# The opening of a four-layer residual chain: token columns and codebook spread by TensorE, lora_A in two loads, lora_B turned into every eighth column

## The reference

```python
x = x + (x @ W0.T + b0 + coeff[:, None, None] * einsum('bsi,bio->bso', x, 2 * mask - 1))
delta = lora_B @ lora_A * 0.5                  # lora_B 1024x64, lora_A 64x1024
cb = codebook / max(abs(codebook))             # 8 levels
normalized = (weight + delta) / exp(scale_log) # by groups of 128 columns
quantized = cb[searchsorted(thresholds, normalized)]
x = x + x @ (quantized * exp(scale_log) + delta).T
x = x + x @ W2.T + b2 + (x @ A2[tok2]) @ B2[tok2] * 2
x = x + (x @ B3[tok3].T) @ A3[tok3].T
```

## Time and profile before

| | us |
|---|---|
| median of 3 runs (lowest to highest) | 549.82 (549.53 to 550.76) |
| profiled execution, its own time | 549.87 |
| its span, first to last instruction | 548.2 |
| PE busy in the span | 533.4 (97%) |
| DVE busy | 468.8 (86%) |
| ACT busy | 341.7 (62%) |
| POOL busy | 192.9 (35%) |

### The profile page before, as it was taken

The page is one execution under the profiler, slowest core; times in us unless marked ns, Lnnn a source line. Parts: engine busy times, 40 slices in busy tenths (PEclk is TensorE's granted clock), DMA queues, the critical chain, the costliest instruction groups (busy, mean ns, idle before and its releaser), DMA issues.

```text
span 548.2 us, 8917 instructions
## 1 busy us (share of the span) xinstructions
PE 533.4 (97%) x2856; PEld 454.1 (83%) x2856; DVE 468.8 (86%) x723; ACT 341.7 (62%) x658; POOL 192.9 (35%) x179
## 2 busy tenths in 40 slices
PE   5999999999999999999999999999999999999997
PEld 4988888888888787887888788788888878878886
DVE  5998898988865879977999989998997998999862
ACT  3777776776745874586566657557566665755720
POOL 2669867987734020012034204111410420411130
PEclk9999999999999999999999999999999999999999
DMA  8766041843486995558456545645835654664122
GB/s 232 244 92 148 21 125 48 248 138 115 102 186 189 348 326 100 189 157 171 138 161 167 123 160 175 114 155 189 172 134 168 167 126 158 180 103 168 61 59 77
DMA packets 145261, 84.06 MB, mean 153 GB/s; under 512 B 102672, under 2 KB 118032, under 8 KB 145104
## 3 DMA queue, kind: packets, MB, share of 16 engines
q1 hardware_dynamic: 143312, 78.97, 52.4%
q0 software_dynamic: 1632, 4.72, 3.4%
q10 hardware_dynamic: 288, 0.01, 0.0%
HBM read 67.43 MB, written 16.25 MB: 153 GB/s over the span
## 4 chain that ended last, share of the span: by engine, by line
PE 83%; DVE 9%; ACT 4%; DMA 3%; issue 1%; POOL 0%; DVEq 0%; ACTq 0%; SPq 0%; POOLq 0%
PE bank L1637 19%; PE bank L1644 10%; PE bank L1676 7%; PE bank L1677 7%; PE bank L1675 7%; PE bank L1511 5%; PE bank L1513 5%; PE bank L1512 5%; PE bank L1726 3%; PE bank L1725 3%; PE bank L1727 3%; PE bank L1691 3%; PE bank L1421 2%; PE bank L1704 1%; DVE w_lo L1074 1%; DVE merged_ring L1168 1%
## 5 line engine op out<-in xcount | busy, mean ns | idle before, releaser
L1637 PE MATMUL bank<-x_t_pair,m_hi 128*128 128x512 f32 x512 | 128.5, 393 | 1.5 <-ACT m_hi L800 1.4
L800 ACT CAST m_hi<-merged_ring 128x512 fp32r<-128x512 f32 x128 | 73.1, 619 | 60.7 <-PE bank L1644 31.9
L1637 PEld LDWEIGHTS bank<-x_t_pair,m_hi 128*128 128x128 f32 x512 | 92.5, 189 | 19.2 <-ACT m_hi L800 2.3
L1174 DVE TENSOR_TENSOR m_lo<-merged_ring,m_hi 128x512 fp32r<-128x512 f32 x128 | 86.3, 720 | 12.5 <-ACT m_hi L800 12.2
L576 POOL TENSOR_TENSOR x_t_pair<-x_sum,x_t_pair 128x256 fp32r<-128x256 f32 x32 | 29.7, 960 | 179.1 <-ACT x_t_pair L861 179.1
L1168 DVE TENSOR_TENSOR merged_ring<-merged_ring,w_t 128x1024 f32<-128x1024 f32 x64 | 82.1, 1311 | 11.3 <-ACT merged_ring L790 10.3
L790 ACT ACTIVATE merged_ring<-mask_ring,batch_now 128x1024 f32<-128x1024 int32 x64 | 78.0, 1241 | 21.1 <-DMA mask_ring<-in_mask_Bx4096x_ik 20.3
L1644 PEld LDWEIGHTS bank<-x_t_pair,m_lo 128*128 128x128 f32 x512 | 69.8, 190 | 5.0
L1644 PE MATMUL bank<-x_t_pair,m_lo 128*128 128x256 f32 x512 | 71.4, 282 | 0.0
L1676 PE MATMUL bank<-P_lo,x_t_pair 128*128 128x512 f32 x160 | 62.3, 389 | 0.0
L1675 PE MATMUL bank<-P_hi,x_t_pair 128*128 128x512 f32 x160 | 62.3, 389 | 0.0
(11 more groups left out here) (211 smaller groups left out, 1133.5 us busy)
## 6 DMA issues: line engine op xcount, KB each, us to landing
mask_ring<-in_mask_Bx4096x_ik SPq DMA_DIRECT2D x64, 512.0 KB, 4.4
w_nat<-in_L_cond_W SPq DMA_DIRECT2D x14, 512.0 KB, 5.3
x_t_squares<-in_x SPq DMA_DIRECT2D x56, 128.0 KB, 3.0
w_raw<-in_L_cond_weight SPq DMA_DIRECT2D x16, 256.0 KB
out<-out_staged SPq DMA_DIRECT2D x16, 256.0 KB, 4.5
w0t_dram<-w_out SPq DMA_DIRECT2D x14, 256.0 KB, 2.6
g_batch<-g_dram POOLq DMA_DIRECT2D x28, 128.0 KB, 4.3
w_t<-w0t_dram SPq DMA_DIRECT2D x6, 512.0 KB, 5.1
```

Of the source, the lines that this page charges most:

```text
L800: nc.scalar.copy(Mh[:, n % MR], ring_f[:, k % MR, h * HALF:(h + 1) * HALF]).then_inc(s["h_set"], 1)
L1174: nc.vector.tensor_tensor(Ml[:, n % MR], ring_f[:, k % MR, h * HALF:(h + 1) * HALF], Mh[:, n % MR].bitcast(F32), ALU.subtract).then_inc(s[ ...
L1637: mm(bank[L0_BANK[HT * h + j]][:, :], Mh[:, n % MR, j * P:(j + 1) * P], xThl[:, :, :, k + i, :], start=(k + i == 0), stop=False, skip_grou ...
```

## The change

In words, queue by queue:

- SP: lora_B is loaded with eight consecutive rows for each partition, so each partition gets one run of 2 KB. Of lora_A only the first 128 columns are loaded next; the rest comes after W2's first block, followed by two small loads of the tokens into one partition (for the register reads). The codebook and the scale are no longer loaded here, so the first W1 group stands third.
- ACT: four DMA issues in place of two: tokens as two columns of 8 partitions, the scale, and the codebook into one partition.
- POOL: the identity, a second small mask (`own_t`, 8 partitions) and the number tables come first, then the wait for `rows_set` 2 and the gather; `own` is made after the gather.
- DVE: one more memset (a row of ones), one operation on the token columns, one addition after TensorE has spread them, and a copy of the codebook out of PSUM. The old row arithmetic (two masks, two sums) goes.
- PE: eight transposes of the identity, the product that spreads the token offsets, the product that spreads the codebook, then lora_B: 16 plain products (eight for each half) with 64 moving columns of the identity, each written to every eighth column of a bank, in place of eight transposes of 128 columns. Three identity transposes follow. `delta(0)` waits for the first copy only, `delta(1)` for the second. Eight identity transposes stand before `w2_transpose(0)`, and `w2_transpose(1)` moves ahead of the two `b3_transpose`.
- ACT's order: `w2_hi(1)` and `mid_up(0)` move ahead of the two `b3_set`.

```diff
-            sp.dma_start(lbn[:, :, :], lora_b.rearrange("(t p) r -> p t r", p=P)).then_inc(s["lora_b_in"], 16)
-            sp.dma_start(la[0:RL, :], lora_a).then_inc(s["lora_a_in"], 16)
-            sp.dma_start(cb[:, :], row(codebook).broadcast_to([P, NCB])).then_inc(s["cb_in"], 16)
-            sp.dma_start(sc[:, :, :], scale_log.rearrange("(t p) g o -> p t (g o)", p=P)).then_inc(s["sc_in"], 16)
+            sp.dma_start(lbn[:, :, :], lora_b.rearrange("(p t) r -> p t r", t=KT)).then_inc(s["lora_b_in"], 16)
+            sp.dma_start(la[0:RL, 0:P], lora_a[:, 0:P]).then_inc(s["lora_a_in"], 16)
             for h in range(2):
                 sp.dma_start(raw[:, h], w1_cols[h, 0]).then_inc(w1_in[h], 16)
             for t in range(KT):
+                if t == 1:
+                    sp.dma_start(la[0:RL, P:D], lora_a[:, P:D]).then_inc(s["lora_a_rest"], 16)
+                    for i, v in enumerate((tok2, tok3)):
+                        sp.dma_start(tok[0:1, i], row(v)).then_inc(s["tok_in"], 16)
...
+            nc.gpsimd.memset(own_t[:, :, :], 1.0).then_inc(s["ident_zero"], 1)
...
+            pool.wait_ge(s["ident_zero"], 2)
+            nc.gpsimd.affine_select(out=own_t[:, :, :], in_=own_t[:, :, :], compare_op=ALU.is_equal, fill=0.0, base=0,
+                                    pattern=[[-1, NB], [0, R]], channel_multiplier=1).then_inc(s["ident_set"], 1)
+            nc.gpsimd.iota(batch_off[:, :], pattern=[[0, 2]], base=0, channel_multiplier=-R).then_inc(s["numbers_set"], 1)
+            nc.gpsimd.iota(row_no[:, :], pattern=[[0, 1]], base=0, channel_multiplier=1).then_inc(s["numbers_set"], 1)
+
+            pool.wait_ge(s["rows_set"], 2)
+            nc.gpsimd.indirect_dma_start(b3n[:, :], None, bb3.rearrange("s r n -> (s r) n"),
+                                         bass.IndirectOffsetOnAxis(rows[:, 1:2], 0)).then_inc(s["b3_in"], 16)
+            nc.gpsimd.memset(own[:, :, :], 1.0).then_inc(s["own_set"], 1)
...
             for i, v in enumerate((tok2, tok3)):
-                act.dma_start(tok[:, i], v.rearrange("(o n) -> o n", o=1).broadcast_to([P, NB])).then_inc(s["tok_in"], 16)
+                act.dma_start(tok_col[:, i:i + 1], v.rearrange("(n o) -> n o", o=1)).then_inc(s["tok_col_in"], 16)
+            act.dma_start(sc[:, :, :], scale_log.rearrange("(t p) g o -> p t (g o)", p=P)).then_inc(s["sc_in"], 16)
+            act.dma_start(cb_row[:, :], codebook.rearrange("(o n) -> o n", o=1)).then_inc(s["cb_in"], 16)
...
             inner_up(0)
+            w2_hi(1)
+            mid_up(0)
             b3_set(0)
             b3_set(1)
-            w2_hi(1)
-            mid_up(0)
...
-            dve.wait_ge(s["tok_in"], 32)
+            dve.wait_ge(s["tok_col_in"], 32)
             dve.wait_ge(s["numbers_set"], 2)
...
+            nc.vector.scalar_tensor_tensor(out=slot_off[:, :], in0=tok_col[:, :], scalar=float(R), in1=batch_off[:, :],
+                                           op0=ALU.mult, op1=ALU.add).then_inc(s["rows_set"], 1)
+            dve.wait_ge(s["spread"], 1)
+            nc.vector.tensor_tensor(rows[:, :], bank[2][:, 0:2], row_no[:, 0:1].broadcast_to([P, 2]), ALU.add).then_inc(s["rows_set"], 1)
+
+            dve.wait_ge(s["spread"], 2)
+            link(nc.vector.tensor_copy(cb[:, :], bank[7][:, 0:NCB]))
...
+            def keep_busy(n):
+                for _i in range(n):
+                    nc.tensor.transpose(bank[0][:, 0:P], ident[:, :], ident[:, :])
+
+            keep_busy(8)
+            pe.wait_ge(s["ident_set"], 2)
+            pe.wait_ge(s["rows_set"], 1)
+            mm(bank[2][:, 0:2], own_t[:, :, :].rearrange("b c r -> b (c r)"), slot_off[:, :], start=True, stop=True).then_inc(s["spread"], 1)
+            pe.wait_ge(s["ub_zero"], 2)
+            pe.wait_ge(s["cb_in"], 16)
+            mm(bank[7][:, 0:NCB], one_row[:, :], cb_row[:, :], start=True, stop=True).then_inc(s["spread"], 1)
             pe.wait_ge(s["lora_b_in"], 16)
             for h in range(2):
-                for t in range(HT):
-                    ins = nc.tensor.transpose(bank[5 + h][0:RL, t * P:(t + 1) * P], lbn[:, h * HT + t, :], ident[:, :])
+                spread = bank[5 + h][0:RL, :].rearrange("r (p t) -> r t p", t=KT)
+                half = slice(h * 64, (h + 1) * 64)
+                for t in range(KT):
+                    ins = mm(spread[:, t], lbn[:, t, :], ident[:, half], start=True, stop=True)
                 ins.then_inc(s["lbt_tr"], 1)
+            keep_busy(3)
...
-                elif n == 0:
-                    pe.wait_ge(s["lbt_set"], 2)
+                elif n < 2:
+                    pe.wait_ge(s["lbt_set"], n + 1)
+                elif n == 2:
+                    pe.wait_ge(s["lora_a_rest"], 16)
...
+            keep_busy(8)
             w2_transpose(0)
+            w2_transpose(1)
             b3_transpose(0)
             b3_transpose(1)
-            w2_transpose(1)
```

More of the change, by code:

```diff
@@ L195, in cond_resid_chain @@
     tok = const("tokens", [P, 2, NB], I32)
-    batch_off = const("batch_offset", [P, NB], I32)
+    tok_col = const("token_cols", [NB, 2], I32)
+    batch_off = const("batch_offset", [NB, 2], I32)
     row_no = const("row_number", [P, 1], I32)
-    slot_off = const("slot_offset", [P, 2, NB])
-    slot_own = const("slot_own", [P, 2])
+    slot_off = const("slot_offset", [NB, 2])
+    own_t = at("own_batch_t", [NB, NB, R], F32, reg_ring + 8 * KB)
+    one_row = at("one_row", [1, P], F32, reg_ring + 9 * KB)
+    cb_row = const("codebook_row", [1, NCB])
     rows = const("table_rows", [P, 2], U32)
@@ L209, in cond_resid_chain @@
         s = {n: sem(n) for n in """cb_in sc_in late_in lora_b_in lora_a_in w1_in0 w1_in1 a2_in b2_in a3_in b3_in w0_in w0_in2 w0_out_st0 w0_out_st1 g_stored y_stored
-            ub_in b2row_in x_in0 x_in1 g_in recip_set first_level tok_in b2c_in b2col_set numbers_set rows_set ident_set ident_zero own_set ub_zero
+            ub_in b2row_in x_in0 x_in1 g_in recip_set first_level tok_in b2c_in b2col_set numbers_set rows_set ident_set ident_zero own_set lora_a_rest tok_col_in spread ub_zero
             lbt_tr lbt_set w2_tr w2_hi w2_lo b3_tr b3_set b2_tr b2_set v_done v_hi v_lo bb_done a3_tr a3_set ga_done ab_hi ab_lo b3b2_set y_set gsum_set scale_set cb_set coef_set ga_hi ga_lo
@@ L482, in _ @@
             nc.gpsimd.memset(ident[:, :], 0.0).then_inc(s["ident_zero"], 1)
-            nc.gpsimd.memset(own[:, :, :], 1.0).then_inc(s["own_set"], 1)
+            nc.gpsimd.memset(own_t[:, :, :], 1.0).then_inc(s["ident_zero"], 1)
             pool.wait_ge(s["ident_zero"], 1)
@@ L493, in _ @@
                                     pattern=[[R, NB], [0, R]], channel_multiplier=-1).then_inc(s["own_set"], 1)
-            nc.gpsimd.iota(batch_off[:, :], pattern=[[-R, NB]], base=0, channel_multiplier=0).then_inc(s["numbers_set"], 1)
-            nc.gpsimd.iota(row_no[:, :], pattern=[[0, 1]], base=0, channel_multiplier=1).then_inc(s["numbers_set"], 1)
-            pool.wait_ge(s["rows_set"], 1)
-            nc.gpsimd.indirect_dma_start(b3n[:, :], None, bb3.rearrange("s r n -> (s r) n"),
-                                         bass.IndirectOffsetOnAxis(rows[:, 1:2], 0)).then_inc(s["b3_in"], 16)
             step = Order(pool, s["pool_step"])
@@ L927, in _ @@
             nc.vector.memset(now_tab[:, :, :], 0.0).then_inc(s["ub_zero"], 1)
+            nc.vector.memset(one_row[:, :], 1.0).then_inc(s["ub_zero"], 1)
             nc.vector.memset(la[RL:P, :], 0.0).then_inc(s["lora_pad"], 1)
             nc.vector.memset(lbt[RL:P, :], 0.0).then_inc(s["lora_pad"], 1)
-            dve.wait_ge(s["tok_in"], 32)
+            dve.wait_ge(s["tok_col_in"], 32)
             dve.wait_ge(s["numbers_set"], 2)
-            for i in range(2):
-                step.did(nc.vector.scalar_tensor_tensor(out=slot_off[:, i], in0=tok[:, i], scalar=float(R), in1=batch_off[:, :], op0=ALU.mult, op1=ALU.add))
-            dve.wait_ge(s["own_set"], 3)
-            step.wait()
-            for i in range(2):
-                step.did(nc.vector.tensor_tensor(slot_off[:, i], slot_off[:, i], own[:, :, 0], ALU.mult))
-            step.wait()
-            for i in range(2):
-                step.did(nc.vector.reduce_sum(slot_own[:, i:i + 1], slot_off[:, i], AXX))
-            step.wait()
-            nc.vector.tensor_tensor(rows[:, :], slot_own[:, :], row_no[:, 0:1].broadcast_to([P, 2]), ALU.add).then_inc(s["rows_set"], 1)
-            dve.wait_ge(s["cb_in"], 16)
+            nc.vector.scalar_tensor_tensor(out=slot_off[:, :], in0=tok_col[:, :], scalar=float(R), in1=batch_off[:, :],
[4 more added lines that the diff above has]
+            link(nc.vector.tensor_copy(cb[:, :], bank[7][:, 0:NCB]))
             link(nc.vector.tensor_scalar(cbn[:, :], cb[:, :], -1.0, None, ALU.mult))
@@ L1132, in half @@
                     dve.wait_ge(s["bb_done"], 1)
+                    dve.wait_ge(s["own_set"], 3)
```

## The result

| us | before | after |
|---|---|---|
| median of 6 runs (lowest to highest) | 550.38 (549.53 to 551.37) | 556.02 (554.33 to 557.59) |
| profiled execution, and its span | 549.87, 548.2 | 556.73, 555.0 |

The ratio is 1.0103, its 95% interval 1.0082 to 1.0124. The changed kernel is slower by 5.6 us. The forecast was 551.3, with a range up to 552.9: the sign was right, the time outside the range.

What follows compares the result with a forecast made beforehand. VectorE was taken as the bound from `terms_a(0)` on, the end moving with its start: PE ends lora_B at 9.85, plus 4.8 gives 14.65, 1.5 us late; 549.8 + 1.5 = 551.3 us, range 548.6 to 552.9.

Steps and rivals of the forecast that it cites:

- the term zero for the order swap: PE and ScalarE order: moving `w2_transpose(1)` and `w2_hi(1)` ahead gains zero, as VectorE is already busy.
- rivals 1 to 4: Alternatives: rival 3, Rival 1, Rival 2, and a fourth, slack in VectorE drawing all toward 549.8, no chance of its own.
- PE's start on lora_B: Opening, PE: first lora_B product at about 6.2 us, against 5.88 before, waiting for the codebook landing at 6.1.
- rival 3: Codebook load held up behind the scale to 7.7 us, `terms_a(0)` 3.1 us later, 552.9; chance 0.15.
- lora_B's load: Opening load in 2 KB runs: 4.0 us from issue to landing in place of 4.8, there at about 5.0.
- The turn: PE turning lora_B: 32 instructions, cost by columns, 3.75 us at the lower clock, against 1.89 for the old turn.
- The clock: PE in the opening: lower level when lora_B comes, rising at 9.7 us; identity transposes buy nothing by the skill's rule.
- Rival 1: Clock up when lora_B comes or soon after: 32 instructions in 1.95 us, 549.6 or 548.6; chance 0.25 for over 1.1 us.
- The fixed tail: From the end of PE's lora_B work through copy, exponent, reciprocal and thresholds to `terms_a(0)`: unchanged, 4.8 us.
- The gather: Gather of B3 rows: issued at about 5 in place of 7.38, B3 landing some 2 us earlier; gain zero.
- VectorE then without gaps, and all later steps shifted by as much: After the opening: the later start of `terms_a(0)`, 1.5 us, reappears unchanged in all later steps.
- Rival 2: About even: clock rises halfway, or codebook at 5.2 with a slow turn, +0.65, 550.5; chance 0.27.

Runs made afterwards that it cites:

- a1: The changed kernel with the old order of steps restored on both TensorE and ScalarE; 553.59 us, ratio 1.0056 to the kernel before.
- b1: The kernel before with the order swap alone, on both engines; 553.42 us, ratio 1.0047.
- b2: The kernel before with the swap, but `mid_up(0)` left behind the two `b3_set` on ScalarE; 550.52 us, ratio 1.0008.
- c1: a1 with the codebook load issued ahead of the scale load on ScalarE's queue; 551.58 us, ratio 1.0029.
- a3: The changed kernel with its 19 identity transposes replaced by plain f32 products (4, 2 and 4); 554.81 us, ratio 1.0077.
- a2: The changed kernel with all 19 identity transposes removed; 556.38 us, ratio 1.0108.
- d3: The kernel before with eight plain identity products (16 instructions) at PE's start; 551.96 us, ratio 1.0009.
- d1: c1 with the scale's exponent ahead of lora_B's copies and plain products in place of the identity transposes; 551.68 us, ratio 0.9998.
- a4: The changed kernel with only `mid_up(0)` moved back behind the two `b3_set` on ScalarE; 555.78 us, ratio 1.0093.
- c2: a1 with lora_B turned by eight transposes as before, its 2 KB load kept, ScalarE's copies writing every eighth column; 554.08 us, ratio 1.0064.
- c3: c2 with c1's order of loads and the scale's exponent ahead of the two copies; 553.13 us, ratio 1.0048.
- d2: d1 with b2's order and two plain products in place of the last four; 551.44 us, ratio 1.0000.

## Why the prediction was wrong

**The step that failed** is the term zero for the order swap: the prediction says that moving `w2_transpose(1)` and `w2_hi(1)` ahead gains zero, and the sum has no cost for it either. I had looked at what the two moved steps could win and not at what their move puts behind them. On ScalarE `mid_up(0)` moved too, ahead of `b3_set`; it waits for VectorE's third term, `v_part(0)` waits for `b3_set`, `w2_transpose(2)` stands behind `v_part(0)`, and VectorE needs its result. Undoing the swap wins 2.4 us (a1), doing it alone costs 3.0 (b1), and taking `mid_up(0)` out of the way removes all but 0.5 of that (b2). It stood in the diff, and rivals 1 to 4 had no case for it.

**A second term was mis-sized: PE's start on lora_B.** I had named the right releaser, the codebook, and taken its landing at 6.1 with an upper end of 7.7. It landed at 6.50 and its product ran at 6.64, so lora_B's products began at 7.13 instead of 6.2. Of these 0.93 us, 0.40 are the later landing, a quarter of what rival 3 had (6.1 to 7.7). The other 0.53 are the product that spreads the codebook: from landing to the first lora_B product the sum had 0.1 us, and it took 0.63 (the two instructions at 6.64 last 0.56). By the rule cited from the Trainium skill ("DMA: Bandwidth & Descriptors", queues, rings and completion order) the landing would have been at 7.7; the trace has 6.50, between that and the sum's 6.1. c1 shows that the place behind the scale is the cause of the late landing: in front of the scale's small pieces the same load is there before 4.2, and PE starts 2.4 us earlier. Its landing behind the scale also varies: 5.71 in a3.

**The other terms, in the order of the prediction:**

- lora_B's load: 2.7 us from issue to landing, forecast 4.0. PE waits for the codebook then, so this wins nothing in the change; in c1 it does.
- The turn: 32 instructions in 3.67 us, forecast 3.65 to 3.75. Right, and so is the cost by columns (0.115 each).
- The clock: not up when lora_B comes, right. Rival 1 is out. The identity transposes buy nothing (a2), as argued; d3 shows the other half, which the rows of before could not: plain products do raise it (deltas 2.02 in place of 3.75). Whether it is their kind or their length is not shown: d3 has 3.78 us of them, the change 1.97 us of transposes, and a3, with 2.07 us of plain products, left lora_B's products at 3.67 too. The Trainium skill's rule that the full rate does not engage for transpose-mode work ("TensorE: Matmul & The Clock Gate", Part 4) fits a2, but no run has transposes for as long as d3's products. Behind other work at the upper level, transposes do run at it: eight take 1.04, against that rule as worded, and the measurement decides. My reading that the clock was up by about 12 in before was early: of the eight transposes from 12.09, the first five start 0.21 apart, to 12.94. The sum used it for 0.1 us only.
- The fixed tail: 10.80 to 15.92 is 5.1 us, forecast 4.8. One threshold operation (L962) took 0.45 in place of 0.17, which a1 does not repeat; otherwise the steps are those named, the exponent at 11.34, the reciprocal released by it at 11.68.
- `terms_a(0)`: 15.92, forecast 14.65. Of the 1.27 missing, 0.93 is the start on lora_B (0.40 the landing, 0.53 the spreading product) and 0.3 the tail.
- The gather, forecast to be issued two us earlier and B3 to land as much earlier: half wrong. It is issued at 5.17 in place of 7.38, but takes 9.3 us in place of 7.3, and lands no sooner (14.47, and 14.68 in before). In a1 that costs nothing; once PE comes to `b3_transpose` earlier (c1, d1, and d3 with before's gather), it is the next wait, 1.7 to 2.2 us.
- "VectorE then without gaps, and all later steps shifted by as much": right for the opening's part. In a1 the shift is 2.5 at the first `terms_a`, 2.1 at the third and at the second stage. In after it was false, because of the swap: 2.8, then 6.0.
- Rival 1's gain had no sum of its own behind it: I gave 5.4 as the lower end of the codebook's landing, but rivals 1 and 2 use 5.0 and 5.2. With 5.4 and the upper clock PE would have ended lora_B at 7.45, short of the 7.25 that a gain over 1.1 us needed.
- Rival 2, about even, did not come; c1, nearest to it, is 1.5 us slower than before. That the change does what it says held; that it shortens the opening did not.

What the clock's fall itself costs is less certain than the rest. Between a1 and after (3.9 us at the third `terms_a`) the waits and the slow instructions come together; a4 took out one wait and kept the fall. The whole of the order's effect is shown; its division, some 2.0 us of waiting and 1.5 of clock, is an estimate from a3's one profiled execution.

## What to carry to other kernels

When a step is moved ahead in an in-order queue, list what now stands behind it and what it waits for, to the second and third consumer; a step moved along "for free" can hold up the one that feeds the bound. When a wait disappears from a profile, ask which load is last then: a tiny load behind a many-piece one in the same queue is late by the pieces. An opening shortened by a microsecond is only worth that once the next data (here the gathered rows) are early as well.

## What the runs showed of the hardware

**Waits for loads late in the run differ from trace to trace by as much as the differences measured.** At the start of the second stage ScalarE waits for mask loads (3.6 us in before and 5.6 in d1, from 160 to 200 us), and PE for ScalarE. The PE waits of before in 160 to 300 us, then those of d1:

```profile
PE bank L1637 <- ACT m_hi L800: 1.4, 3, 0.9
```

```profile
PE bank L1662 <- ACT m_hi L811: 3.4, 3, 2.0
```

In the table this is the step from first to last `m_hi`: 343.4 us in before, 344.3 in after, 345.2 in a1, 345.8 in d1. So the 0.9 us by which after grows in the second stage, and 1.8 of a1's, arise far behind the opening. Each kernel has one trace, so whether such a wait belongs to the kernel or to the execution is not shown. In the same way c2, c3 and a2 have a wait of 1.2 to 1.8 us for a weight load (`w_nat`) in the first stage that a1 and before do not have; with the mask waits it accounts for c2 and c3 standing worse at 521 than at 35 us. c3's four runs (551.9, 552.2, 554.1, 554.2) may differ by it. The profiled executions of a2, c3, d1 and d2 were the slowest or among the slowest of their kernels, c1's was the fastest, so the place where such a wait first appears says more than the end.

**The granted clock falls behind short holes here.** Idle stretches of PE of 3.18 us (a2), 2.56 (a4), 2.36 (after), 2.28 (b1), 2.15 (d3) and 2.10 (d1) were followed by windows at 0.50. Those of 1.15 (before), 1.33 and 2.28 (a3's profiled execution), 1.63 (d2) and 1.74 (c1) were not. All of them have transposes before or behind them, so these do not tell the two groups apart. The falls lasted between 3 and 7 us and took a group of eight transposes from 1.04 to 1.9 us and after's `v_part(0)` from 2.05 to 3.6.

**A strided write costs ScalarE.** The copy of 64x512 f32 from PSUM took 0.59 us to contiguous columns and 1.0 us to every eighth column (c2, c3). As matmul output the same stride cost nothing that shows: 0.115 us for 64 columns at the lower level, half of the 0.234 for 128 contiguous ones.
